# Top-3 expert layer: results scaled before they are stored, then gathered with an adding DMA

## The reference

```python
an = _rmsnorm(attn_out, gamma2)
shared = gelu(an @ sh_w1 + sh_b1) @ sh_w2 + sh_b2
logits = an @ router_w + router_b                 # 31 experts
aff = softmax(logits)
topv, topi = top_k(aff, 3)
gates = sum(one_hot(topi, 31) * topv[..., None], axis=-2)
h = gelu(einsum('bsd,edh->besh', an, re_w1) + re_b1)
routed = einsum('bse,besh,ehd->bsd', gates, h, re_w2) + einsum('bse,ed->bsd', gates, re_b2)
return shared + routed + an + attn_out
```

## Time and profile before

| | |
|---|---|
| median of 3 runs | 1054.77 us (1049.03 to 1056.14) |
| the profiled execution's own time | 1058.01 us |
| its span | 1055.9 us |
| TensorE busy | 934.4 us (88%) |
| VectorE busy | 672.3 us (64%) |
| ScalarE busy | 547.1 us (52%) |
| GpSimd busy | 478.1 us (45%) |
| mix, last part (ranks and lists) | 811 to 850 us in the span |
| experts | 850 to 1056 us |

### The profile page before, as it was taken

How to read it: one execution, slowest core, us unless ns; L and a number is a source line. 1 busy time by engine, 2 the same in 40 slices (tenths; PEclk the granted TensorE clock), 3 DMA queues, 4 the chain that set the end, 5 groups by cost and what they waited for, 6 DMA issues and landing times. The chain is left out here.

```text
span 1055.9 us, 19030 instructions
## 1 busy us (share of the span) xinstructions
PE 934.4 (88%) x5522; PEld 690.8 (65%) x5522; DVE 672.3 (64%) x2043; ACT 547.1 (52%) x1371; POOL 478.1 (45%) x613
## 2 busy tenths in 40 slices
PE   7979998997989899669999999998997769999973
PEld 4655555654757576457776776766885359999951
DVE  5865675672796888567777776651554845333366
ACT  5647886783342434357777777661233125555520
POOL 6013573543887878711123332242410056444675
PEclk9989999997999999979999999998998779999975
DMA  7658657433668758889777778727796035446854
GB/s 236 213 168 235 195 179 179 148 107 120 239 227 297 260 207 305 296 218 251 185 200 194 201 204 218 188 72 195 244 299 197 1 96 158 134 135 127 156 169 129
DMA packets 148022, 200.21 MB, mean 190 GB/s; under 512 B 21370, under 2 KB 89753, under 8 KB 147922
## 3 DMA queue, kind: packets, MB, share of 16 engines
q1 hardware_dynamic: 136162, 175.36, 54.8%
q0 software_dynamic: 6048, 16.52, 7.2%
q10 hardware_dynamic: 5712, 7.13, 2.2%
HBM read 121.37 MB, written 77.46 MB: 188 GB/s over the span
## 5 line engine op out<-in xcount | busy, mean ns | idle before, releaser
L990 DVE CUSTOM_DVE_ANT_0 a_sm<-a_sc,keep_mask_qk 128x512 f32<-128x512 f32 (+3 forms) x256 | 118.2, 482 | 65.0 <-PE a_sc L906 58.2
L721 DVE CUSTOM_DVE_ANT_0 rope_x<-a_sc,keep_mask_qk 128x512 bf16<-128x512 f32 (+3 forms) x256 | 112.0, 487 | 56.8 <-PE a_sc L616 50.2
L978 ACT ACTIVATE a_probs<-a_sm,a_neg 128x512 f32<-128x512 f32 (+3 forms) x256 | 140.1, 552 | 8.4 <-DVE a_neg L990 8.4
L1853 POOL DMA_INDIRECT ex_y<-an,keep_ids x78 | 75.6, 969 | 133.9 <-POOLq L61 75.1
L905 PE MATMUL a_sc<-a_ka,a_qa 128*128 128x512 f32 (+3 forms) x256 | 96.9, 379 | 26.4 <-POOL a_ka L887 20.0
L887 POOL CAST a_ka<-a_ka 64x512 fp32r<-64x512 f32 x64 | 38.9, 608 | 177.6 <-DMA a_qa<-qs 176.9
L1281 POOL TENSOR_TENSOR rope_rot<-rope_wqkv 128x512 f32<-128x512 f32 x64 | 94.3, 1489 | 33.1 <-DVE rope_wqkv L1346 33.0
L911 PE MATMUL a_tp<-keep_ident,a_probs 128*128 128x128 f32 x640 | 105.3, 281 | 0.0
L911 PEld LDWEIGHTS a_tp<-keep_ident,a_probs 128*128 128x128 f32 x640 | 75.2, 142 | 25.6 <-issue 17.4
L1987 DVE COPY ex_w<-keep_w 128x514 f32 x78 | 33.7, 432 | 90.5 <-ACT ex_hid L1937 87.9
L1231 PE MATMUL p_ub<-rope_km,rope_wh 128*128 128x512 f32 x256 | 82.0, 402 | 6.0 <-DVE rope_km L1336 6.0
(11 more groups left out here) (269 smaller groups left out, 2106.2 us busy)
## 6 DMA issues: line engine op xcount, KB each, us to landing
a_qa<-qs SPq DMA_DIRECT2D x128, 128.0 KB, 4.1
ks<-rope_rot SPq DMA_DIRECT2D x40, 256.0 KB, 3.1
qs<-rope_rot SPq DMA_DIRECT2D x40, 256.0 KB, 2.1
ye<-ex_ysb SPq DMA_DIRECT2D x78, 128.0 KB
rope_qm<-qs SPq DMA_DIRECT2D x64, 128.0 KB
rope_km<-ks SPq DMA_DIRECT2D x64, 128.0 KB
qs<-rope_qm SPq DMA_DIRECT2D x32, 256.0 KB, 2.6
vs<-rope_vout SPq DMA_DIRECT2D x16, 512.0 KB, 3.3
```

The lines of the kernel that those rows point to most:

```text
L721: return dve.tensor_tensor_reduce(out=junk[:, JUNK[qb]:JUNK[qb] + n], in0=src, in1=c.mask_qk[:, S - n:S], scale=1.0, scalar=-3e38, op0=ALU ...
L978: act.activation(probs[:, h % PR, rows(qb)], sm[:, h % SM, rows(qb)], ACT.Exp, bias=neg[:, h % 2, qb:qb + 1], scale=-1.0, accum_out=sums[: ...
L990: return dve.tensor_tensor_reduce(out=sm[:, h % SM, rows(qb)], in0=src[:, 0:n], in1=c.mask_qk[:, S - n:S], scale=-1.0, scalar=3e38, op0=AL ...
```

## The change

1. **Gates travel with the tokens.** `mix` turns the logits into the full gate matrix by batch: the new function `gates(b)` on VectorE (four instructions), with one exponential per batch on ScalarE instead of one at the end. The tensor `an` gets 31 more columns, and SyncE stores the gates there (`store_gates`, four DMAs). A gather of `an` brings 287 numbers a row instead of 256.
2. **Rows are scaled before they are stored.** VectorE picks the column of the tile's expert (`scale`, one small copy per tile), and ScalarE's copy of the result multiplies by it (L1997).
3. **The order of a token's choices.** In `experts` VectorE sorts the three places of every token. For sorted choice k and token tile i, the largest place decides how many tiles must be stored. TensorE and VectorE work these bounds out in iterations 2 to 41. For this input the bounds of k = 0 are 55, 46, 47, 53, 44, 52, 52, 50, 36, 27, 45, 44, 50, 56, 51 and 57 tiles; those of k = 1, by groups of four token tiles, are 58, 60, 61 and 61; k = 2 waits for all 62.
4. **The gathers of results add.** 48 gathers (L1909) go straight into `c.base[:, i]` with an add in the DMA, all 16 of k = 0 first, then k = 1, then k = 2. Each waits for the one before it on the same token tile. The multiply-adds on VectorE are gone; it adds the bias alone.
5. **Buffers and layout.** The first gathers have a ring of their own with 32 slots instead of 12. `ye` is laid out by tile ("(n p)") instead of by partition. The bias products have eight PSUM banks and all can be made at once.

```diff
 def mix(nc, c, t):
+            def store_gates(b):
+                sp.wait_ge(gated, b + 1)
+                sp.dma_start(t["an"][P * SB * b:P * SB * (b + 1), D:D + E].rearrange("(s p) e -> p s e", p=P),
+                             c.logits[:, SB * b:SB * b + SB, :]).then_inc(gates_out, 16)
...
                 if b + 1 < B:
                     pre(b + 1)
-            act.wait_ge(spread_in, B)
-            act.activation(c.ex[:, :, :], logit_d[:, :, :], ACT.Exp).then_inc(exped, 1)
-            act.activation(c.top_ex[:, :, :], top_d[:, :, :], ACT.Exp).then_inc(exped, 1)
+                act.wait_ge(spread_in, b + 1)
+                cols = slice(SB * b, SB * b + SB)
+                act.activation(c.logits[:, cols, :], logit_d[:, cols, :], ACT.Exp).then_inc(exped, 1)
...
+            def gates(b):
+                cols = slice(SB * b, SB * b + SB)
+                ex = c.logits[:, cols, :]
+                dve.wait_ge(exped, b + 1)
+                then(dve.tensor_reduce(ex_sum[:, 0, cols], ex, AX.X, ALU.add))
+                tick.add(dve.tensor_tensor(ex, ex, member[:, cols, :], ALU.mult))
+                then(dve.reciprocal(ex_sum[:, 1, cols], ex_sum[:, 0, cols]))
+                dve.tensor_tensor(ex, ex, over_experts(ex_sum[:, 1, cols], SB), ALU.mult).then_inc(gated, 1)
...
             choose(B - 1)
+            gates(B - 2)
...
+            gates(B - 1)
             dve.wait_ge(placed, 1)
 def experts(nc, c, t, out):
...
-            tiles = pool.value_load(c.experts[0:1, P - 1:P], min_val=TOK * TOPK // P, max_val=NT)
-            pool.wait_ge(ye_done, tiles)
-            pool.wait_ge(gate_ready, 1)
-            for i in range(TILES):
-                if i == FREE:
-                    pool.wait_ge(turned, NT)
-                ge(pool, summed, ADDS * (i - RING + 1))
-                for k in range(TOPK):
-                    pool.indirect_dma_start(out=y[:, i % RING, k, :], out_offset=None, in_=t["ye"],
...
+            pool.wait_ge(slots_ready, 1)
+            pool.wait_ge(bounds_ready, 1)
+            pool.wait_ge(base_whole, 2)
+            for k in range(TOPK):
+                for i in range(TILES):
+                    if k == 0:
+                        tiles = pool.value_load(bound_i[0:1, i:i + 1], min_val=FEWEST, max_val=NT)
...
+                        pool.wait_ge(ye_done, tiles)
+                        pool.nop(nofuse=True)
+                    ge(pool, landed[i], 16 * k)
+                    pool.indirect_dma_start(out=c.base[:, i, :], out_offset=None, in_=t["ye"],
+                                            in_offset=bass.IndirectOffsetOnAxis(ap=c.slots[:, k, i:i + 1], axis=0),
+                                            compute_op=ALU.add).then_inc(landed[i], 16)
...
-                    act.activation(ysb[:, n % YR, :], yb[n % 2][:, 0:D], ACT.Copy).then_inc(y_copied, 1)
+                    act.activation(ysb[:, n % YR, :], yb[n % 2][:, 0:D], ACT.Copy, scale=scale[:, n % YR, 0:1]).then_inc(y_copied, 1)
...
                 dve.wait_ge(turned, r + 1)
+                ge(dve, y_copied, r - YR + 1)
+                dve.tensor_copy(scale[:, r % YR, 0:1], slot(r)[:, D:D + E][:, bass.ds(e, 1)])
                 dve.tensor_copy(xT[:, r % 2, :, :].rearrange("p k n -> p (k n)"), tb[r % 2][:, 0:DC * P]).then_inc(x_copied, 1)
...
             for i in range(TILES):
-                dve.wait_ge(fetched[i % RING], 16 * TOPK * (i // RING + 1))
-                for k in range(TOPK):
-                    ge(dve, summed, ADDS * i + k)
-                    dve.scalar_tensor_tensor(out=c.base[:, i, :], in0=y[:, i % RING, k, :], scalar=c.gates[:, i, k:k + 1],
-                                             in1=c.base[:, i, :], op0=ALU.mult, op1=ALU.add).then_inc(summed, 1)
-                dve.wait_ge(b_mul, i + 1)
-                dve.wait_ge(summed, ADDS * i + TOPK)
-                dve.tensor_add(c.base[:, i, :], c.base[:, i, :], bb[i % 2][:, 0:D]).then_inc(summed, 1)
+                dve.wait_ge(b_mul, 2 * (i // 2) + 2)
+                dve.wait_ge(landed[i], 16 * TOPK)
+                dve.tensor_add(c.base[:, i, :], c.base[:, i, :], bias_bank(i // 2)[:, D * (i % 2):D * (i % 2) + D]).then_inc(biased, 1)
```

More of the change, by code:

```diff
@@ L1399, in mix @@
         row_noh = a.sb("row_noh", [P, P], F16)
-        pos, part = a.sb("pos", [P, TOPK, TILES]), a.sb("part", [P, TOPK, TILES])
+        pos, part = c.pos, a.sb("part", [P, TOPK, TILES])
+        row, tile_no = (a.sb(n, [P, TOPK, TILES]) for n in ("row", "tile_no"))
+        oh, ex_sum = a.sb("oh", [P, TOPK, TILES, E]), a.sb("ex_sum", [P, 2, TILES])
         RING = 8
@@ L1759, in _ @@
                     logits(b - 1)
+                if b >= 2:
+                    gates(b - 2)
                 outputs(b)
@@ L1788, in _ @@
             for k in range(TOPK):
-                n = tick.add(dve.tensor_tensor(picked[:, k, :, :], c.oh[:, k, :, :], ranks, ALU.mult))
+                n = tick.add(dve.tensor_tensor(picked[:, k, :, :], oh[:, k, :, :], ranks, ALU.mult))
             dve.wait_ge(tick_s, n)
@@ L1793, in _ @@
             then(dve.tensor_scalar(part[:, :, :], pos[:, :, :], 1.0 / P, (P - 1) / (2.0 * P), ALU.mult, ALU.subtract))
-            then(dve.tensor_scalar(c.tile_no[:, :, :], part[:, :, :], ROUNDER, ROUNDER, ALU.add, ALU.subtract))
-            then(dve.scalar_tensor_tensor(out=c.row[:, :, :], in0=c.tile_no[:, :, :], scalar=-float(P), in1=pos[:, :, :],
+            then(dve.tensor_scalar(tile_no[:, :, :], part[:, :, :], ROUNDER, ROUNDER, ALU.add, ALU.subtract))
+            then(dve.scalar_tensor_tensor(out=row[:, :, :], in0=tile_no[:, :, :], scalar=-float(P), in1=pos[:, :, :],
                                           op0=ALU.mult, op1=ALU.add))
@@ L1847, in tile, with slot, bias_bank @@
             return 0 <= n < NT
+        def slot(q):
+            return ring[:, q % RING, :]
+        def bias_bank(j):
+            return (bb + hb + yb + tb)[j]
         @block.gpsimd
@@ L1860, in _ @@
[L1860 to L1867 removed]
+                ge(pool, x_copied, n - RING + 1)
@@ L1963, in close_mix, with aside @@
-            def close_mix(r):
-                dve.wait_ge(closing, r)
+            tick = Tally(tick_s)
+            p0, p1, p2 = (c.pos[:, k, :] for k in range(TOPK))
+            def aside(r):
                 if r < 2:
                     half = c.base[:, TILES - SB + 2 * r:TILES - SB + 2 * r + 2, :].rearrange("p i d -> p (i d)")
-                    dve.tensor_add(half, half, c.last[r]).then_inc(closing, 1)
+                    dve.tensor_add(half, half, c.last[r]).then_inc(base_whole, 1)
@@ L1973, in close_mix @@
                 elif r == 4:
-                    dve.tensor_tensor(c.gates[:, :, 0:TOPK], c.top_ex[:, :, :],
-                                      inv[:, :].rearrange("p (i o) -> p i o", o=1).to_broadcast([P, TILES, TOPK]), ALU.mult)\
-                       .then_inc(closing, 1)
+                    dve.tensor_tensor(key[:, 1, :], high[:, :], middle[:, :], ALU.min)
+                    dve.tensor_tensor(key[:, 2, :], high[:, :], middle[:, :], ALU.max).then_inc(keyed, 1)
                 elif r == 5:
-                    dve.scalar_tensor_tensor(out=slotf[:, :, :], in0=c.row[:, :, :], scalar=float(NT), in1=c.tile_no[:, :, :],
-                                             op0=ALU.mult, op1=ALU.add).then_inc(closing, 1)
-                elif r == 6:
-                    dve.tensor_copy(c.slots[:, :, :], slotf[:, :, :]).then_inc(closing, 1)
+                    dve.wait_ge(keyed, 1)
```

141 lines of the change are left out of this document (80 added, 61 removed).

## The result

| | before | changed |
|---|---|---|
| median | 1051.90 us (4 runs, 1044.57 to 1056.14) | 1085.42 us (4 runs, 1079.71 to 1086.97) |
| ratio | | 1.0295, 95% interval 1.0263 to 1.0327 |
| profiled execution, its span | 1058.01, 1055.9 us | 1085.85, 1084.1 us |
| first and last gather of results start | 987.45, 1047.73 | 986.21, 1074.68 |
| from one such gather to the next | 1.28 us | 1.88 us |

The kernel became 3.0% slower, where 1% faster was forecast, and the time lies outside the range. A ratio is always the time of a kernel over that of the kernel before, taken on the same chip; an interval that doesn't hold 1 is clear of noise. A few executions showed a far lower clock and a much longer time (1285.98 us beside 1042.87, for one), and medians and ratios leave them out.

What follows compares the result with a forecast made beforehand. GpSimd's rate, 48 gathers at 1.28 us each, was taken to bound the end. The terms -13.9 - 1.6 + 0 + 0 + 1.6 = -13.9 us took 1054.8 to 1041 us; likeliest case 1037 to 1047, wide range 1037 to 1076.

Steps and rivals of the forecast that it cites:

- The adding gather itself: The 48 gathers of results on GpSimd: adding costs no more than plain, 0 us; upper bound +0.95 us each.
- d: Extra us per adding gather on GpSimd, paid 48 times; gain gone at 0.29, slower by 1% from 0.51.
- rival A: At the 48 gathers: adding costs GpSimd far more, kernel slower; chance 0.24 of over 0.51 us extra each.
- Loop: Loop over tiles: column copies, scaling and sorting lie beside TensorE, wider rows and `ye` layout have slack; 0 us.
- mix: Before the ranks: later `x1` load and `gates(3)` after the last exponential cost +1.6 us, +6.4 with the slowest landing.
- End: After the last gather's landing: three multiply-adds go, only the bias stays, -1.6 us.
- Earlier start: First gather of results waits for 55 stored tiles instead of 62, so the series starts 13.9 us sooner.
- Rival D: Gathers of results do not start sooner: bounds one too high or ring holds GpSimd; 1043 to 1055 us, chance 0.05.
- Register loads: 21 loads between GpSimd's gathers, run ahead of time by its sequencer: 0 us, +16.8 if it cannot.
- rival C: GpSimd's sequencer cannot run ahead, so 21 register loads stand in the open: +16.8, 1058 us, chance 0.10.
- Rival B: DMA engines, not GpSimd, set the pace of the adding gathers: +10.8, 1052 us, chance 0.12.

## Why the prediction was wrong, step by step

The forecast in the profiled execution was a span of 1055.9 - 13.9 = 1042.0 us. The changed kernel's is 1084.1, 42.1 more. The steps account for all of it.

- **The adding gather itself: taken at 0, it cost 28.2 us.** This is the step that failed. From first to last gather 47 x 1.882 = 88.5 us instead of 47 x 1.283 = 60.3. d was 0.60 us, above the 0.51 at which rival A makes the kernel slower by 1%, and its mechanism is what happened. I had both ends (0 and 0.95; 48 x 0.95 is 45.6 us, not the 45.4 of the prediction) and took the lower with the argument that the nearest row is the plain gather. For an operation that the trace doesn't show, on the engine that sets the end and 48 times over, the nearest row gives the lower bound and no more. The add's price was measured by leaving out one keyword: 28.0 us went with it. Rival A's 1086 us for twice the descriptor time matches the result only by chance: at d = 0.60 the same sum gives 1041 + 28.8 = 1070, and three other losses filled the rest. The Trainium skill (Collectives: The Full Stack, The bandwidth ceiling: the fold count and why AG ≠ RS ≠ AR) has two read descriptors for the adding step of a collective, where a copy has one. Worked out as a share of GpSimd's time this estimate came to +0.47 us, near the 0.60, but the runs speak against that reading: half the rows take off 0.13 us, so the price isn't one of descriptors by row.
- **Loop: taken at 0, it cost 8.4 us.** The ring of 32 slots was read as a gain without a price ("only transfers with slack"). It let GpSimd gather the empty tiles' one row every 1.32 us; the stores behind them made ScalarE, and so TensorE, wait. Three waits of TensorE hold 5.8 of the 8.4 us; from 960 to 980 us its granted clock was 0.91 and not 1.00. The trace of before had the warning: the share of the DMA engines stood at 0.97 from 970 to 990 us in the row shown above, against 0.45 from 940 to 960, at no more data. I had read the earlier trace rows at 880 to 920 and not there. Time from the ranks to the first gather: 155.9 us, where the kernel before has 987.45 - 826.07 = 161.4, less the 13.9 of the early start, 147.5.
- **mix: taken at +1.6, it was +4.2.** The ranks came at 830.27 instead of 826.07. `x1` landed 8.8 us after its request, near the 9.7 of the earlier trace rows and not the 3.9 that I took. I argued that the same load among the same neighbours would be as quick, but the neighbours had changed: at 804.19 the request went out ahead of SyncE's store of `an` and its two loads of weights of 896 KB each (807.20 and 807.62), and at 811.19 it stood behind them (807.06 and 808.02). That these are what slowed it wasn't tested apart; asked for at 803.96 again, `x1` was there in time. The other part, `gates(3)`, was right: with the load out of the way 1.6 us stay.
- **End: taken at -1.6, it was +1.3.** From the last gather's start to the end of the span 9.4 us instead of 8.2. The three multiply-adds are gone as said, but the landing is 1.2 us longer, GpSimd's drain ends 1.4 us after SyncE's last wait, and the last 0.2 or 0.3 lie behind the drain. The drain wasn't in my sum. It isn't the adds' doing: with plain gathers in the same places it ended 6.5 us behind the last descriptors too, against 4.9 in the kernel before. Why is open.
- **Earlier start: -13.9, right.** With the hole gone the first gather starts 146.8 to 147.6 us after the ranks in three kernels, against the 147.5 worked out, so the bounds come out as the choices say. Rival D is out.
- **Register loads: 0, right.** Gaps of 0.30 us with and without them, so rival C is out. They had been run through ahead of time: the last one stood at 1024.3, with gathers going out until 1074.68. The loads took 0.28 to 0.76 us. The Trainium skill (DMA: Bandwidth & Descriptors, Latency and other measured facts) gives about 600 ns as a floor; the median of sixteen here is 0.29, and none of them showed.
- **Rival B (pace of the DMA engines)** is out for the adding gathers: the gap stays 0.30, the landing 3.8 to 4.6 us, and the share in the last 44 us is 0.60. Its worry was right at another place, the gathers of the empty tiles.

In all: 28.2 + 8.4 + (4.2 - 1.6) + (1.3 + 1.6) = 42.1 us.

## What to carry to other kernels

Where one engine's rate of issuing sets the end, an instruction of a new form in its stream is the whole question: measure one such instruction before anything is built on it, and until then price it from its known relative upward only. A deeper ring doesn't only bring data sooner, it sets the pace at which transfers fall on the DMA engines, so look for the stretch of the old trace where their share is already near 1. And a rewrite of several parts is best tried without the dubious one: here sorting and early start were worth 1%, with the adds left on an engine that had 5 of 20 us to spare.

## What the runs showed of the hardware

- An indirect gather that adds into SBUF occupied GpSimd for 1.30, 1.42 and 1.55 us at 16, 64 and 128 rows of 1 KB, a plain one 0.84, 0.90 and 0.95. The width of the rows didn't matter (plain 0.94 at 512 bytes; adding 1.640 at 512 bytes and 1.638 at 1 KB, for the same sixteen). The values at 16 and 64 rows are from one execution each. What the fixed 0.45 us consist of stays open.
- The adding gathers wrote three times as many packets to the queue's record for the same 6.29 MB: 6912 for 48 of them, 2304 for 48 plain ones. They landed 3.9 us after their start, plain ones 3.0.
- Gathers that read one row of memory 128 times load the DMA engines far more than ones with different rows: a share of 0.97 against 0.44, at 133 and 136 GB/s. At one gather each 1.98 us that was hidden, at one each 1.32 us it cost 8.4 us. Why one row is slower no run shows.
- GpSimd's drain at the end of the block closed 4.9 us behind its last descriptors in the kernel before, ahead of the end of SyncE's wait. It closed 6.2 us behind its last descriptors in the changed kernel and 6.5 us with plain gathers there, later than SyncE's wait for the last output both times.
